# A graph network of four layers: the graph layers' work placed among the attention's row groups

## What is computed

```python
def L0(x, adj, W, b):
    adj = adj + eye(N); d = sum(adj, -1) ** -0.5
    return (d[:, :, None] * adj * d[:, None, :]) @ x @ W.T + b
def L1(x, adj, WQ, WK, p):
    mask = where(adj > 0, 0.0, -1e22)
    q = x @ WQ; k = x @ WK
    h = relu(q[:, None, :, :] + k[:, :, None, :])
    score = einsum('bijd,d->bij', h, p)
    return softmax(score + mask, -1) @ x
def L2(x, adj, W, b):
    adj = adj + eye(N); d = sum(abs(adj), -1) ** -0.5
    return (d[:, :, None] * adj * d[:, None, :]) @ (x @ W) + b
def L3(x, adj, W, b):
    d = 1.0 / sqrt(sum(adj, 2) + 1e-8)
    return (d[:, :, None] * adj * d[:, None, :]) @ x @ W + b
for L in (L0, L1, L2, L3):
    x = layernorm(x + L(x, adj, ...))
```

## Time and profile before

| | |
|---|---|
| median of 3 runs | 15444.7 us (15443.2 to 15445.18) |
| the profiled execution | 15425.52 us |
| its span, first to last instruction | 15423.3 us |
| granted TensorE clock, mean | 0.974 of full speed |
| DVE, PE, ACT, POOL busy | 91%, 86%, 83%, 5% |
| DMA, mean over the span | 38 GB/s |

### The profile page before, as it was taken

The page is one execution under the profiler, slowest core; times in us unless marked ns, Lnnn a source line. Parts: engine busy times, 40 slices in busy tenths (PEclk is TensorE's granted clock), DMA queues, the critical chain, the costliest instruction groups (busy, mean ns, idle before and its releaser), DMA issues. The chain is left out here.

```text
span 15423.3 us, 363837 instructions
## 1 busy us (share of the span) xinstructions
PE 13297.8 (86%) x152965; PEld 6323.3 (41%) x152965; DVE 13958.6 (91%) x14776; ACT 12757.3 (83%) x7764; POOL 773.4 (5%) x863
## 2 busy tenths in 40 slices
PE   7888888888888888888888888888888888888888
PEld 4333453334533355333553335433354333543335
DVE  7999779997799977999779997899978999789996
ACT  6999769996699966999669996699966999679995
POOL 0000000000000000000000000000000000000000
PEclk9999999999999999999999999999999999999999
DMA  2000120001200012000120002100021000210001
GB/s 98 13 10 13 67 86 13 10 13 67 86 13 13 10 72 80 13 13 10 76 77 13 13 10 82 71 13 13 13 87 63 13 13 13 95 54 12 12 12 53
DMA packets 128454, 579.53 MB, mean 38 GB/s; under 512 B 27536, under 2 KB 61328, under 8 KB 61328
## 3 DMA queue, kind: packets, MB, share of 16 engines
q1 hardware_dynamic: 126864, 554.28, 9.4%
HBM read 411.63 MB, written 142.61 MB: 36 GB/s over the span
## 5 line engine op out<-in xcount | busy, mean ns | idle before, releaser
L658 DVE TENSOR_SCALAR big<-q_pair,supp 128x2048 f32<-128x2048 f32 x10240 | 12302.8, 1280 | 42.7 <-PE score L891 35.8
L446 ACT ACTIVATE big<-q_f,k_f 128x2048 f32<-128x2048 f32 x6144 | 11758.2, 1996 | 694.1 <-PE score L891 681.4
L891 PE MATMUL score<-big,unit_window 128*32 128x512 f16 x81920 | 5335.8, 399 | 1773.9 <-DVE big L658 1522.6
L891 PE MATMUL score<-big,sign_window 128*32 128x512 f32 x49152 | 5615.4, 597 | 0.0
L891 PEld LDWEIGHTS score<-big,unit_window 128*32 128x32 bf16 x81920 | 2157.2, 97 | 4926.1 <-DVE big L658 2111.5
L891 PEld LDWEIGHTS score<-big,sign_window 128*32 128x32 f32 x49152 | 1607.8, 111 | 3113.6 <-issue 2832.1
L828 PE MATMUL acc<-supp,big 128*128 128x128 f32 x12288 | 1445.9, 275 | 30.3 <-ACT supp L402 29.0
L828 PEld LDWEIGHTS acc<-supp,big 128*128 128x128 f32 x12288 | 1406.4, 192 | 34.7 <-ACT supp L402 19.9
L386 ACT ACTIVATE x_turned<-turn 128x512 f32<-128x512 f32 x64 | 38.6, 603 | 1028.8 <-PE turn L783 971.6
L368 POOL TENSOR_SCALAR att_var<-att_mom 128x1 f32<-128x1 f32 x128 | 146.3, 1143 | 12870.3 <-DVE att_mom L635 12870.3
L556 DVE TENSOR_TENSOR agg<-acc,supp 128x512 f32<-128x512 f32 x64 | 44.3, 692 | 654.6 <-PE acc L828 654.6
(11 more groups left out here) (98 smaller groups left out, 2868.9 us busy)
## 6 DMA issues: line engine op xcount, KB each, us to landing
att<-in_adj_dram SPq DMA_DIRECT2D x160, 1024.0 KB, 4.8
adj_turned<-big SPq DMA_DIRECT2D x128, 1024.0 KB, 11.3
big<-adj_turned SPq DMA_DIRECT2D x128, 1024.0 KB, 18.0
q_f<-in_adj_dram SPq DMA_DIRECT2D x32, 1024.0 KB, 10.3
q_pair<-in_adj_dram SPq DMA_DIRECT2D x32, 1024.0 KB, 10.1
k_f<-in_adj_dram SPq DMA_DIRECT2D x32, 1024.0 KB, 10.4
xin<-in_x_dram SPq DMA_DIRECT2D x128, 64.0 KB, 1.8
out_dram<-xatt SPq DMA_DIRECT2D x32, 256.0 KB, 2.9
```

Source lines behind the costliest of these rows:

```text
L446: ins = nc.scalar.activation(ring["A"][:, RANK[g] % RING * 4 + u, :], q_f32[:], ACT.Relu, bias=k_f32[:, bass.ds(t * P + (QUAD * u + g), 1)])
L658: ins = nc.vector.tensor_scalar(ring["D"][:, RANK[g] % RING * 4 + u, :], q_pair[:], k_pair[:, bass.ds(t * P + (QUAD * u + g), 1)], None, A ...
L891: ins = nc.tensor.matmul(score[QUAD * u:QUAD * (u + 1), c, :], window[:, QUAD - 1 - g:2 * QUAD - 1 - g], row, start=(g == 0 and part == 0) ...
```

## The change

**New order.** Each engine's program is written out over 512 places per attention pass, 16 blocks of 32 row groups, and `side(c, place)` adds at fixed places what used to stand between attentions. The pass of index c has the rows of batch c + 1, layers 2 and 3 of batch c, and the half tiles, layer 0, q and k of batch c + 2. There are eight passes: the first has no layers 2 and 3, the last no half tiles and no layer 0. Ahead of the first pass stand, without rows, the turning of batch 0 and its layer 0, q and k; behind the last, layers 2 and 3 of batch 7. All loops are unrolled.

**Turning.** A tile of the adjacency (128 x 2048) is taken as two half tiles, 32 per batch, one every 10 places from place 2 on. `raw` has a single buffer. With the place of a half tile as 0: PE turns four blocks at 0 and four at 3, ACT copies at 3 and 6, DVE sums at 4, ACT sums absolute values at 7, SP stores at 7 and loads the next half tile at 8.

**Graph layers.** The turned adjacency is no longer held. It is streamed from DRAM in pieces of 128 x 512 (256 KB), 64 per layer, through four buffers. The input of a layer is scaled first for all nodes (`gs`), its bias added (`gx`), two DVE operations of 128 x 2048 each. The product is formed turned: one 512-wide matmul per piece with `gs` as the weights, 16 of them in 26 places, then ACT copies it (place 30 of the step), PE multiplies with the layer's weights (36), DVE adds and takes statistics (40), POOL the root (41), DVE writes the output (46). A step starts every 30 places, from 42 (layer 2), 182 (layer 3) and 336 (layer 0). The term of the unit matrix, an addition on DVE before (L556), is four matmuls with `ident` (`add_self`). q and k and their pairs of halves go to DRAM step by step and are loaded at a pass's start; k comes per block. x after the attention is kept in DRAM as well. The negation of the maximum is part of the reduction now. `raw_abs_summed` and the sums are per half.

```diff
-    adj_turned = nc.dram_tensor("adj_turned", (B * T, P, N), F32, kind="Internal").ap()
...
+    UNITS = 2 * T
+    PIECES = 4
...
+    PLACES = T * GROUPS
+    UNIT_AT, UNIT_EVERY = 2, 10
+    BASE = {"layer2": 42, "layer3": 182, "layer0": 336}
+    SCALE_AT = {"layer2": 38, "layer3": 179, "layer0": 332}
+    STEP_EVERY = 30
+    PIECE_AT = {(i * 26) // T: i for i in range(T)}
+    EYE_AT, TURNED_AT, PROJECT_AT, SUM_AT, ROOT_AT, NORM_OUT_AT, STORE_AT = 23, 30, 36, 40, 41, 46, 47
...
+    adj_turned = nc.dram_tensor("adj_turned", (B * STEPS * T, P, BANK), F32, kind="Internal").ap()
...
+            def load_raw(c, u):
+                b = c + 2
...
+                else:
+                    sp.wait_ge(turn_full[1], turn_use(c, ("unit", u - 1, 1)) + 1)
+                    sp.wait_ge(raw_summed, unit_of(b, u))
+                    sp.wait_ge(raw_abs_summed, unit_of(b, u))
+                sp.dma_start(raw[:], half_rows(b, u)).then_inc(raw_loaded, 16)
...
+            def load_piece(c, name, s, i):
+                n = piece_of(c, name, s, i)
+                if not one_of(c, OPENING) or n >= PIECES:
+                    sp.wait_ge(piece_used, piece_of(c, name, s, i, 1 - PIECES + AHEAD))
+                b = {"layer2": c, "layer3": c, "layer0": c + 2}[name]
+                sp.dma_start(piece[:, i % PIECES, :], adj_turned[b * (STEPS * T) + (s * T + i)]) \
+                    .then_inc(piece_loaded[i % PIECES], 16)
...
+            def sum_unit(c, u):
+                dve.wait_ge(raw_loaded, unit_of(c + 1, u) * 16 + 16)
+                if u == 0:
+                    dve.wait_ge(degrees_ready, c + 2)
+                nc.vector.tensor_reduce(deg_part[:, u % 2, u // 2:u // 2 + 1], raw[:], AX.X, ALU.add) \
+                    .then_inc(raw_summed, 1)
...
+                nc.vector.tensor_tensor(gs[:], gx[:], dis[name].unsqueeze(2).broadcast_to([P, T, D]), ALU.mult) \
+                    .then_inc(gs_ready, 1)
+                dve.wait_ge(gs_ready, layer_of(c, name) + 1)
+                nc.vector.tensor_tensor(gx[:], gx[:],
+                                        bias[name][:].rearrange("p (a f) -> p a f", a=1).broadcast_to([P, T, D]),
+                                        ALU.add).then_inc(biased, 1)
...
-            def graph_layer(b, stage, arrived, beside=None):
...
-                    for j in range(PER):
-                        t = s * PER + j
-                        for m in range(T):
-                            ins = nc.tensor.matmul(acc[k][:, j * P:(j + 1) * P], big[:, t, m * P:(m + 1) * P],
-                                                   supp[:, m, :], start=(m == 0), stop=(m == T - 1))
...
+            def turn_unit(c, u, k):
+                if k == 0:
+                    pe.wait_ge(raw_loaded, unit_of(c + 1, u) * 16 + 16)
+                pe.wait_ge(turn_free[1], turn_use(c, ("unit", u, k)) + AHEAD)
+                turn_four(1, lambda j: raw[:, (k * PER + j) * P:(k * PER + j + 1) * P])
...
+            def add_piece(c, name, s, i):
+                n = piece_of(c, name, s, i)
+                if i == 0:
+                    if s == 0:
+                        pe.wait_ge(gs_ready, layer_of(c, name) + 1)
+                    pe.wait_ge(layer_turned, step_of(c, name, s) + AHEAD)
+                pe.wait_ge(piece_loaded[i % PIECES], layer_of(c, name) * (STEPS * T // PIECES * 16) +
+                           (s * (T // PIECES) + i // PIECES + 1) * 16)
+                nc.tensor.matmul(acc[1][:], gs[:, i, :], piece[:, i % PIECES, :], start=(i == 0), stop=(i == T - 1)) \
+                    .then_inc(piece_used, 1)
...
+            def side(c, place):
+                for u in units_at(c, place, 0):
+                    turn_unit(c, u, 0)
+                for u in units_at(c, place, 3):
+                    turn_unit(c, u, 1)
+                for name, s in steps_at(c, place, PROJECT_AT):
+                    project(c, name, s)
+                queries_keys(c, place)
+                for name in side_layers(c):
+                    for s in range(STEPS):
+                        at = place - BASE[name] - STEP_EVERY * s
+                        if at == EYE_AT and name != "layer3":
+                            add_self(s)
+                        if at in PIECE_AT:
+                            add_piece(c, name, s, PIECE_AT[at])
...
+                    side(c, place)
+                    score_rows(block_of(c, t), g)
...
+            attention(FIRST)
+            for c in range(B - 2):
+                attention(c)
+            attention(LAST)
```

More of the change, by code:

```diff
@@ L36, in build @@
     GROUPS = QUAD
-    assert D == P and T % 2 == 0
+    assert D == P and T % 2 == 0 and B > 2
     N_ACT = 12
@@ new lines, in attention @@
+            def attention(c):
+                for place in range(PLACES):
+                    t, g = divmod(place, GROUPS)
+                    if g == NORM_AT and (t > 0 or not one_of(c, FIRST)):
+                        att_root(c * T + (T + t - 1))
+                    side(c, place)
+            for place in range(PLACES):
+                side(OPENING, place)
+            attention(FIRST)
+            for c in range(B - 2):
+                attention(c)
+            attention(LAST)
+            att_root(B * T - 1)
@@ L416, in _ @@
+            for place in range(PLACES):
+                side(CLOSING, place)
         @block.scalar
@@ L500, in _ @@
-            with act.Fori(0, T // RAW) as h:
-                for i in range(RAW):
-                    turn_block(0, h, i)
-            with act.Fori(0, B - 1) as b:
-                batch(b, True)
-            batch(B - 1, False)
+            for u in range(UNITS):
+                first_unit(u)
+            for place in range(PLACES):
+                side(OPENING, place)
+            attention(FIRST)
+            for c in range(B - 2):
+                attention(c)
+            attention(LAST)
@@ L508, in _ @@
+            exponentials(B * T)
+            for cc in range(CHUNKS):
+                copy_weights(B * T - 1, cc)
+            for place in range(PLACES):
+                side(CLOSING, place)
         @block.vector
@@ L925, in _ @@
[L925 to L931 removed]
+                        if t == 1 and MULTIPLY_AT[g] == 0:
+                            pe.wait_ge(x1_ready, c + 2)
+                        weigh(m, MULTIPLY_AT[g])
+                    side(c, place)
+                    score_rows(block_of(c, t), g)
```

1184 lines of the change are left out of this document (653 added, 531 removed).

## The result

The changed kernel takes 14,536.0 us (median of 4 runs, 14,532.6 to 14,536.8) against 15,444.5 us before (15,443.2 to 15,445.2). The ratio is 0.9412, its 95% interval 0.9400 to 0.9423: 5.9% faster, 76 us above the forecast and inside its range.

A forecast was written before the change was run, and what follows sets the result against it. Bound now by DVE in attention and PE between; in changed blocks with pieces both about equal. Opening 235, first pass 1706, six of 1769, last 1681, closing 200 make 14,436 us span, forecast 14,460 us, range 14,150 to 15,080.

The forecast's parts named there:

- The sum: Whole span: opening 235, first pass 1706, six middle passes of 1769, last 1681, closing 200, giving 14,436 us.
- With a layer and half tiles: Blocks with layer 2 or 3 and half tiles: PE 108.9 us plus 2.4 for waits, 111.3; DVE 109.4.
- A piece: One 128x512 float32 matmul on PE: 0.86 us, 0.96 with a change of shape.
- list of what would be wrong: Piece above 1 us of PE, DVE side operation above its row, or PE at its lower clock level where pieces run.
- The two operations of a scaling: DVE's scaling and bias of a layer's input over 2048 columns: 2.28 us each, 4.6 a layer, 13.8 a batch.
- Half tiles were charged 10 us a batch: Single-buffered half tile's load, landing in 5 to 7 us with two places, 6.8 us, before PE needs it.
- PE was to idle: Sign in blocks with pieces: some 2 us of PE idle per block, before the second or third row group.
- DVE alone: Rival: PE has room and DVE alone decides; blocks 109.4, 108.0 and 105.6 us, total 14,250 us; chance 0.20.
- The slower rival: Single-buffered half tile comes late; gain gone from 4.5 us each, 16,000 us at 6.9 late; chance 0.07 above 15,475.
- The milder form: Half tiles 1.5 to 4 us late each, or 0.3 to 0.6 per piece: 14,800 to 15,400 us; chance 0.13.
- Nothing gained: Rival: side work makes DVE and PE wait for each other as long as the stretches took, 15,440 us; chance 0.02.
- Transfer size: 256 KB pieces at the skill's 64 KB rate: 1.9 us each, hidden in attention, some 180 us in opening and closing.

The follow-up runs named there:

- the kernel with four parts: Changed kernel with both operations of a layer's input scaling and bias written as four 512-column parts at separate places; 14,445.1 us.
- the doubled: Changed kernel with each piece's matmul done twice into the same sum; 15,632.1 us.
- the narrowed pieces: Changed kernel with each piece's matmul taking 128 of its 512 columns, loads, waits, copies and steps kept; 14,207.3 us.
- two buffers: Changed kernel with two buffers for the streamed pieces instead of four; 14,681.0 us.

## Why the prediction was right, point by point

**The sum.** Forecast of span 14,436, measured 14,535, 99 more. Opening 235 forecast, 229.9; first pass 1706, 1707.7; six middle passes 1769, 1785.2 each, +97; last 1681, 1692.1; closing 200, 194.3. The error is all in the passes that have layers 2 and 3.

**Blocks.** With half tiles alone 105.4 forecast, 105 in the first pass. Bare 101.6, now 101.0. With a layer and half tiles 111.3, now 112.7 in the mean of blocks 2, 3, 4, 6, 7 and 8 (111.5 to 113.9). With layer 0, 109.7, now 111.2 (blocks 11 to 13). In the last pass 106.9, now 109.6.

**The terms that were off.** A piece was put at 0.96 us; behind rows, as most are in the stretches read, it is 1.06: at most 1.7 us per block with 17 pieces, which can carry the 1.4 to 1.5 missing above. That is the term of the sum that was mis-sized; a piece above 1 us of PE also stood on the prediction's list of what would be wrong. The two operations of a scaling were priced well (2.28 each, measured 2.29). Half tiles were charged 10 us a batch for a late load and cost nothing. 11 blocks x 1.4 - 10 is +5 a pass, against +16.2 measured. The other 11 are about what the kernel with four parts took off a pass (13.3): the scaling in one place, and PE's clock. The prediction saw danger in that operation only in its price, and it took the clock as staying at 0.98; it is 1.00 in block 2, where PE is full, and 0.94 in block 5. The 10 us charged for half tiles hid as much of these missed costs: so much of the nearness of the sum is luck.

**What each engine waits for.** PE was to idle some 2 us per block with pieces: 1.8 in block 2, but 9.7 in block 1 and 13.4 in block 5, where pieces stand in a part of the block only. DVE was to idle 1 to 2; it is 4 to 6. That follows from PE's longer pieces, at 112.7 us a block against 108.7 of DVE work. The sums on DVE took 1.21 us, forecast 1.2. Their group on the page, and that of the turnings of half tiles (count; busy us, mean ns; idle us ahead):

```profile
L994 PE MATMUL turn<-ident,raw 128*128 128x128 f32 x1792 | 290.6, 285 | 0.0
L774 DVE TENSOR_REDUCE deg_part<-raw 128x1 f32<-128x1024 f32 x224 | 271.0, 1210 | 0.0
```

**The rivals.** DVE alone (14,250) fell, by the doubled and by the narrowed pieces; the latter also shows about what it would have been, 14,207, of which 14 us were saved in opening and closing. The weight loads, which spoke for it, did not tell the two cases apart. The slower rival needed a half tile 4.5 us late. The two rows above have 0.0 us of idle time in front of the turnings and the sums. The prediction put two places, 6.8 us, between load and turning; there are 18.1, of which 12.5 are left. The milder form has the same answer, and the pieces cost PE 9 us of waiting in opening and closing together. Nothing gained fell with the result.

**Transfer size.** The trace has 2.7 us for a piece from issue to landing, and in the closing four in flight fed one per 0.96 us (median, start to start) with 3.4 us of waits in all. The DMA engines, put at about 15%, are 27% busy in block 2, without a wait of PE for a piece among the rows. The Trainium skill's "DMA: Bandwidth & Descriptors", section "Measured", had led the prediction to an estimate of 14,640 us if 256 KB transfers went at its figure for 64 KB. That time was reached only with two buffers (14,681).

## What to carry to other kernels

When two stages are bound by different engines, placing the one among the other's instructions gains up to the shorter stage; here 294.5 us between attentions became 160 us more than the same pass with bare blocks (1785.2 against 16 x 101.6), and what is left is the sum of the work on the engine that is fuller in each block. Count that work from start to start, per block and per engine, with the cost of a change of shape, and not by weight loads. Then look at the place of the side work. Work in a row on DVE (4.6 us for a scaling) cost 2 to 3 us beyond its length in the block where PE had to catch up behind it, and less than 1 us where DVE was the full engine anyway. Where it stood against the host's own work, with the same amount of it, was worth some 90 us of 14,500. And compare the same block in several passes and kernels, with its granted clock, before a difference of 4 us is put down to an edit.

## What the runs showed that I had not expected

- The place of layer 0's work alone, with its amount and order kept, moved the time by 88 us (14,445.1 to 14,533.0), as much as came back when seven eighths of the columns of every half tile's sum on DVE were left out (87 us).
- After two idle gaps of 2.7 and 2.8 us PE ran a row group in 3.38 us where it otherwise takes 1.82, with a granted clock of 0.84 in those 10 us: 1.6 us more behind 5.5 us of waiting.
- The same block of the same program took 112.9 us in one pass and 116.9 in the next, with granted clocks of 0.98 and 0.94.
- A piece costs 0.1 us more behind a row group than behind a turning of four 128-column blocks.
- The queue of SP runs far ahead of the place written for it: 12.5 us of room for the half tile read, where two places of 3.4 us were counted.
